# Later weight casts and subtractions, and batch 0's scores and maxima taken around the last residual product, in a gated cross-attention and expert layer

## What is computed

```python
xn = layernorm(x)
k, v = split((ctx @ W_src.T + b_src) * mask)        # 8 heads of 16
q = (xn @ W_tgt.T + b_tgt) * mask
attn = softmax(where(mask == 0, -inf, q k / 4))      # per batch and head
x = x + tanh(g0) * (concat([xn, attn @ v]) @ W_out.T + b_out)
xn2 = layernorm(x)
s = sigmoid(xn2 @ gate.T + bias)                     # 9 experts, 2 taken per token
out = sum over the 2: weight * (silu(xn2 @ w1[e].T) * (xn2 @ w3[e].T)) @ w2[e].T
return x + tanh(g1) * out
```

## Time and profile before

| what | before |
|---|---|
| median of three runs | 217.67 us |
| span of the profiled execution | 234.1 us |
| TensorE busy | 205.4 us, 88% |
| VectorE busy | 149.6 us, 64% |
| ScalarE busy | 142.7 us, 61% |
| POOL busy | 128.8 us, 55% |

### The profile page before, as it was taken

One profiled execution on the slowest core, in us unless ns is written; L12 is line 12 of the kernel. 1 busy time (PEld: TensorE's weight loads), 2 busy tenths in 40 slices (PEclk: granted clock), 3 DMA queues, 4 the chain that ended last, 5 costly groups with the idle time before them and its releaser, 6 DMA issues.

```text
span 234.1 us, 5788 instructions
## 1 busy us (share of the span) xinstructions
PE 205.4 (88%) x1606; PEld 166.9 (71%) x1606; DVE 149.6 (64%) x523; ACT 142.7 (61%) x399; POOL 128.8 (55%) x230
## 2 busy tenths in 40 slices
PE   8999986999999999898883946299999999999981
PEld 3577653666666676565573945299999999999881
DVE  0469997788898698897865822344443444456774
ACT  2286869988778876786471620266667666666210
POOL 4237745132325876786783578556675756557320
PEclk9999999999999999999998897589999999999998
DMA  5999999999910100011372221121222221261194
GB/s 164 368 377 242 407 381 409 408 370 318 342 55 13 36 23 26 23 36 38 86 214 62 61 76 49 41 53 55 61 69 68 52 65 47 49 218 53 37 348 163
DMA packets 23602, 34.91 MB, mean 149 GB/s; under 512 B 2562, under 2 KB 15879, under 8 KB 23443
## 3 DMA queue, kind: packets, MB, share of 16 engines
q1 hardware_dynamic: 20610, 29.27, 37.9%
q0 software_dynamic: 2240, 4.23, 5.5%
q10 hardware_dynamic: 720, 1.02, 1.5%
HBM read 15.85 MB, written 19.06 MB: 149 GB/s over the span
## 4 chain that ended last, share of the span: by engine, by line
PE 56%; DVE 14%; another core or an unknown queue 7%; ACT 6%; DMA 6%; issue 5%; POOL 4%; SPq 1%; POOLq 0%; DVEq 0%; ACTq 0%
PE pt_ps L1363 10%; PE score_ps L1321 5%; PE pt_ps L1372 4%; PE score_ps L1323 4%; PE score_ps L1322 4%; PE score_ps L1176 4%; DMA kheads<-y_rows 3%; PE pt_ps L1116 3%; PE ps_a L1226 3%; PE pt_ps L1214 3%; PE score_ps L1126 2%; PE ps_b L1283 2%; DVE less L827 2%; ACT probs L401 2%
## 5 line engine op out<-in xcount | busy, mean ns | idle before, releaser
L616 POOL DMA_INDIRECT y_rows<-vals,ids x38 | 37.8, 995 | 17.2 <-ACT vals L473 9.6
L1363 PE MATMUL pt_ps<-w,probsT 128*128 x234 | 34.4, 285 | 14.6 <-ACT probsT L480 6.7
L1363 PEld LDWEIGHTS pt_ps<-w,probsT 128*128 128x128 f32 x234 | 32.1, 198 | 15.9 <-issue 15.8
L593 POOL DMA_INDIRECT x_rows<-stage,slot x32 | 32.7, 1022 | 10.4 <-issue 7.7
L401 ACT ACTIVATE probs<-score_ps,less 128x128 f32<-128x128 f32 x128 | 37.9, 419 | 0.4 <-DVE less L827 0.4
L1043 DVE TENSOR_TENSOR xg_low<-ps_a,xg_high 128x128 fp32r<-128x128 f32 x40 | 11.7, 291 | 37.1 <-issue 23.6
L473 ACT ACTIVATE vals<-pt_ps,xg 128x128 f32<-128x128 f32 x38 | 14.0, 368 | 34.4 <-PE pt_ps L1363 24.7
L1321 PE MATMUL score_ps<-w_high,xg_low 128*128 x80 | 30.3, 379 | 0.0
L1051 DVE TENSOR_TENSOR probs<-probs,score_ps 128x352 f32<-128x352 f32 x40 | 20.8, 521 | 11.2 <-PE score_ps L1323 5.3
L1323 PE MATMUL score_ps<-w_high,xg_high 128*128 x80 | 26.6, 332 | 0.0
L1322 PE MATMUL score_ps<-w_low,xg_high 128*128 x80 | 26.5, 332 | 0.0
(11 more groups left out here) (179 smaller groups left out, 445.6 us busy)
## 6 DMA issues: line engine op xcount, KB each, us to landing
x_rows<-pads SPq DMA_DIRECT2D x1, 9945.0 KB, 37.3
w_low<-in_w13T SPq DMA_DIRECT2D x3, 1056.0 KB, 11.0
xg<-x_rows SPq DMA_DIRECT2D x40, 65.0 KB
ctx_r<-in_ctxT SPq DMA_DIRECT2D x4, 512.0 KB, 7.7
y_rows<-pads SPq DMA_DIRECT2D x1, 2048.0 KB, 16.6
w<-in_w2T SPq DMA_DIRECT2D x1, 1728.0 KB, 11.2
kheads<-y_rows SPq DMA_DIRECT2D x3, 512.0 KB, 5.0
mask_b<-in_mask SPq DMA_DIRECT2D x4, 256.0 KB, 8.0
```

The source lines that it names most:

```text
L593: pool.indirect_dma_start(x_rows[:, :], bass.IndirectOffsetOnAxis(ap=slot[:, par, c, p:p + 1], axis=0), stage[:, par, c, p, :], None, boun ...
L616: pool.indirect_dma_start(y_rows[:, :], bass.IndirectOffsetOnAxis(ap=ids[:, s:s + 1], axis=0), yt[:, s, :], None, bounds_check=last_row, o ...
L1363: last = nc.tensor.matmul(into[:, 0:D], hidT[:, q3, c, :], w2[:, bass.ds(e3, 1), c, :].rearrange("p o d -> p (o d)"), start=(c == 0), stop ...
```

## The change

On ScalarE the casts of experts 4 and 5 go into group 3 ahead of the wait for its keys, and those of experts 6, 7 and 8 to the ends of steps 2, 3 and 4. On VectorE no subtraction is left in the projections: experts 0, 1 and 2 are subtracted in step 1, 3 to 7 in steps 2 to 6, and 8 in step 9. In group 3 TensorE computes batch 0's scores between the query product and the residual product. VectorE takes the first half of batch 0's maxima ahead of the residual addition and the second half behind it, and `spread(3)` follows both.

```diff
+LOWS = {1: (0, 1, 2), 2: (3,), 3: (4,), 4: (5,), 5: (6,), 6: (7,), 9: (8,)}
...
+                if j == NG - 1:
+                    high(4)
+                    high(5)
                 act.wait_ge(k_done, j + 2)
...
-                for e in ((), (0, 1), (2, 3), (4, 5, 6))[j]:
+                for e in ((), (0, 1), (2, 3), ())[j]:
                     high(e)
...
-                if k < 2:
-                    high(7 + k)
+                if 2 <= k < NE - 4:
+                    high(4 + k)
...
                 if j + 1 == NG:
-                    spread(j)
+                    maxima(0, 0, 0)
                 dve.wait_ge(r_mm, j + 3)
                 nc.vector.tensor_tensor(xs[:, here, :], bank[3].rearrange("p (b d) -> p b d", b=UN), xs[:, here, :], ALU.add).then_inc(r_done, 1)
-                if j + 1 < NG:
-                    spread(j)
-                if j >= 2:
-                    low(j - 2)
+                if j + 1 == NG:
+                    maxima(0, 0, 1)
+                spread(j)
...
-                if on(k, 0):
+                if on(k, 0) and k > 0:
                     maxima(k, r, 0)
...
-                if 2 + k < NE:
-                    low(2 + k)
+                for expert in LOWS.get(k, ()):
+                    low(expert)
...
                 nc.tensor.matmul(bank[2], w_tgt[:], xn1T[:, r, :], start=True, stop=True).then_inc(q_mm, 1)
+                if j == NG - 1:
+                    pe.wait_ge(v_done, NG + 1)
+                    pe.wait_ge(k_done, NG + 1)
+                    pe.wait_ge(kh_pool, 2 + 2)
+                    pe.wait_ge(kh_dve, 2)
+                    pe.wait_ge(kh_act, 2 + 2)
+                    pe.wait_ge(bias_set, 1 + 2)
+                    all_scores(0, 0)
                 pe.wait_ge(scaled_w, 1)
...
             def step(k, r, i):
-                if k == 0:
+                if k == 1:
                     pe.wait_ge(q_done, NG + 1)
-                if k == 1:
                     pe.wait_ge(r_done, NG + 1)
...
-                if on(k, 0):
+                if on(k, 0) and k > 0:
                     if after(k, 2):
                         pe.wait_ge(prob, 2 * k - 2)
...
+                    all_scores(k, r)
...
-            pe.wait_ge(v_done, NG + 1)
-            pe.wait_ge(k_done, NG + 1)
-            pe.wait_ge(kh_pool, 2 + 2)
-            pe.wait_ge(kh_dve, 2)
-            pe.wait_ge(kh_act, 2 + 2)
-            pe.wait_ge(bias_set, 1 + 2)
             pe.wait_ge(ld_gate, 16)
             turns(step)
```

More of the change, by code:

```diff
@@ L696, in spread, with maxima @@
                 last.then_inc(kh_dve, 1)
+            def maxima(k, r, half):
+                here = slice(half * UN, (half + 1) * UN)
+                dve.wait_ge(scores, 2 * k + half + 1)
+                nc.vector.tensor_reduce(less[:, r % 2, here], score_ps[:, r % 2, here, :], AX.X, ALU.max, negate=True).then_inc(lessened, 1)
             for j in range(NG):
@@ L821, in label_rows @@
                 nc.vector.tensor_copy(slot[:, g % 2], slot_f[:]).then_inc(label_set, 1)
[L823 to L827, removed]
             def unturn(b, q):
@@ L1159, in queries_and_rest, with score_products, score_bias, all_scores @@
                 last.then_inc(r_mm, 1)
+            def score_products(k, r, pair, half):
+                rows, heads = slice(half * RH, (half + 1) * RH), slice(2 * pair, 2 * pair + 2)
+                nc.tensor.matmul(score_ps[:, r % 2, half * HH + 2 * pair:half * HH + 2 * pair + 2, :], qT[rows, k * P:(k + 1) * P],
+                                 kheads[rows, heads, k * P:(k + 1) * P], start=(pair == 0), stop=False, tile_position=(half * RH, 0),
+                                 skip_group_check=True)
+            def score_bias(k, r, half):
+                rows = slice(half * RH, (half + 1) * RH)
+                nc.tensor.matmul(score_ps[:, r % 2, half * HH:(half + 1) * HH, :], share[rows, :],
+                                 bias_b[rows, k * P:(k + 1) * P].unsqueeze(1).to_broadcast([RH, HH, P]),
+                                 start=False, stop=True, tile_position=(half * RH, 0), skip_group_check=True).then_inc(scores, 1)
+            def all_scores(k, r):
+                for pair in range(2):
+                    for half in range(2):
+                        score_products(k, r, pair, half)
+                for half in range(2):
+                    score_bias(k, r, half)
             values(0)
@@ L1171, in _ @@
                 queries_and_rest(j)
-            def score_products(k, r, pair, half):
-                rows, heads = slice(half * RH, (half + 1) * RH), slice(2 * pair, 2 * pair + 2)
-                nc.tensor.matmul(score_ps[:, r % 2, half * HH + 2 * pair:half * HH + 2 * pair + 2, :], qT[rows, k * P:(k + 1) * P],
-                                 kheads[rows, heads, k * P:(k + 1) * P], start=(pair == 0), stop=False, tile_position=(half * RH, 0),
-                                 skip_group_check=True)
-            def score_bias(k, r, half):
-                rows = slice(half * RH, (half + 1) * RH)
-                nc.tensor.matmul(score_ps[:, r % 2, half * HH:(half + 1) * HH, :], share[rows, :],
-                                 bias_b[rows, k * P:(k + 1) * P].unsqueeze(1).to_broadcast([RH, HH, P]),
-                                 start=False, stop=True, tile_position=(half * RH, 0), skip_group_check=True).then_inc(scores, 1)
             def step(k, r, i):
-                if k == 0:
+                if k == 1:
                     pe.wait_ge(q_done, NG + 1)
-                if k == 1:
                     pe.wait_ge(r_done, NG + 1)
```

## The result

The changed kernel takes 215.4 us (median of six runs, 214.43 to 215.48) against 217.88 for the kernel before (six runs). The ratio is 0.9869, with a 95% interval of 0.9847 to 0.9891: 2.85 us faster, where 1.3 had been forecast.

What follows compares the result with a forecast made beforehand. The bound was taken as the VectorE-then-ScalarE chain of waits where projections hand over to attention, with weight work on it. 1.5 us won at scores 3 less 0.2 in step 9 gave 217.67 - 1.3 = 216.4 us, range 215.4 to 217.6.

Steps and rivals of the forecast that it cites:

- Scores 0, residual product, addition, maxima and exponentials: Start of attention: scores 0 at 31.35 not 32.63, exponentials end 1.6 us earlier, scores 2 at 38.1 not 39.88.
- Three subtractions in step 1: VectorE, step 1: they cost 2.75 us (2.4 to 3.6), delay upd's transpose and give back 0.3 at scores 3.
- Rival B: Step 1: subtractions and POOL's v_cur products exclude each other three times; gain only 0.6, 217.1 us; chance 0.22.
- high(8)'s old place: ScalarE, step 1: removing this cast gives 0.1 us at most, since the transposes are as late; taken 0.
- high(6), (7), (8) in steps 2 to 4: Ends of ScalarE's steps: each cast fits the idleness; bounds 0 and 0.67 us per step, taken 0.
- Rival E: Steps 2 to 4 and step 9: weight work is not hidden; net 1.4 us slower, 219.1 us; chance 0.08.
- low(8) in step 9: VectorE, before step 9's x addition: the subtraction costs 0 to 0.87 us, taken 0.2.
- Sum: Whole kernel: 1.5 us won at scores 3, less 0.2 in step 9, gives 1.3 and 216.4 us.
- rival D: VectorE and POOL interleave well, step 9 free, high(8)'s absence counts: gain 1.8 to 2.2 us; chance 0.12.
- Rival C: Expert stage: a stop ending at a fixed moment absorbs the gain, leaving 217.7 us; chance 0.08.

Runs made afterwards that it cites:

- e4: Only the order of scores 0, residual product, maxima and spread(3) changed against the kernel before, casts and subtractions left; ratio 1.0005.
- e3: Casts and subtractions both moved against the kernel before, order of scores and maxima left as it was; ratio 0.9871.
- e1: Only the casts moved against the kernel before: 4 and 5 ahead of group 3's keys, 6 to 8 to steps 2 to 4; ratio 0.9979.
- e8: As e3, but four subtractions in step 1 and none later than step 6; ratio 0.9874 to the kernel before.
- e5: The kernel before run again unedited, for a second profile; 216.64 us, ratio 1.0008.
- e9: Another profile of the unedited kernel before, mean granted clock 0.986; scores 15 at 72.50 us after group 3's key products.
- e10: Another profile of the unedited kernel before, mean granted clock 0.985; scores 15 at 72.34 us after group 3's key products.
- e13: The kernel before with five idle products of 0.25 us added on TensorE in step 1; ratio 0.9967.
- e11: Another profile of the unedited kernel before, mean granted clock 0.987; 187.6 us from group 3's key products to the end.
- e14: Another profile of the kernel with only the order of scores, residual product and maxima changed, mean granted clock 0.987; 218.86 us.

## Why the prediction was wrong

The direction and the mechanism were right: weight work was on the path where attention starts, and once it was off, the gain made there was kept, 1.82 us at scores 3 and 1.89 at scores 15. Two steps failed: the price of high(8), taken as 0, and TensorE's clock, which was no term. The size was short by 1.5 us. By the steps of the prediction:

- *Scores 0, residual product, addition, maxima and exponentials.* Forecast for scores 2: 38.1 - 28.6 = 9.5 after the key products; measured 9.59. The added wait was there too, scores 1 at 6.14 and not 5.68. But the sum credited the new order with part of this, and e4 and e3 show that it earns nothing; kT without low(0) and the exponentials without casts earn it all. The weight transfer came in time: the casts of experts 4 and 5 started at 30.38. (The prediction's 29.9 for it should be 29.5, 17.5 + 12.0.)
- *Three subtractions in step 1.* Forecast 2.75 for the three; measured 2.78, behind a spreading that took 1.11 on VectorE's timeline beside POOL's addition and not the 0.47 of group 2's, with upd's transpose 12.62 after the key products and 12.7 forecast. The Trainium skill (SBUF — State Buffer, "Who interferes with whom") counts tensor_scalar, which the spreading is, among the operations that can take the port pair that VectorE shares with GpSimd; the trace agrees for the spreading. Rival B's three exclusions did not come: POOL's four products ended at 38.33, in the first subtraction. (Its 3.6 was high even so, 3 x 1.16 is 3.5.)

```profile
35.22 1.26 POOL L538 TENSOR_TENSOR xs<-xs,b_resg 128x512 f32<-128x512 f32 x1 [2.23 <-DVE xs L730]
36.45 1.88 POOL L545 TENSOR_TENSOR v_cur<-vals,factors 128x136 f32<-128x136 f32 x4
```

- *high(8)'s old place, "0.1 at most, taken 0".* This term was mis-sized. It is 0.31 by e1. The prediction looked only at the start of the next copy. The rows of the kernel before showed more: behind the cast the copies and the ulT copy were recorded longer, 0.44 for ulT against 0.27 here. Step 2 is 4.28, where the forecast had 4.7: the cast's 0.31 is gone, and the late transpose costs 0.18 (e3's step is 4.10) and not 0.3.
- *high(6), (7), (8) in steps 2 to 4, taken 0.* Right within 0.06: steps of 4.43, 4.37 and 4.37. Rival E did not happen. The step with high(6):

```profile
44.29:48.66 4.37, 4.37 (x44) 2.98 (x42) 3.63 (x9) 4.37 (x15) 1.49 (x5) 1.00 1.02 402
```

ScalarE is now busy 4.37 of 4.37, against 3.82 in the earlier trace rows, and the loop is hardly longer.

- *low(8) in step 9, taken 0.2.* Measured 0, net: 0.18 lost by scores 12 against e8 and 0.22 back in step 12. VectorE still idled 0.31 before the addition, of the 1.11 in the earlier trace rows.

```profile
73.95 0.88 DVE L693 TENSOR_TENSOR w_low<-w_low,w_high 128x704 fp32r<-128x704 f32 x1
75.14 0.29 DVE L870 TENSOR_TENSOR xs<-ps_b,xs 128x128 f32<-128x128 f32 x1 [0.31 <-PE ps_b L1297]
```

- *Sum.* 1.3 forecast, 1.9 in the program: 0.3 is the cast of step 1, 0.2 is low(8), and some 0.1 the rest. This is rival D, 1.8 to 2.2 with step 9 free and high(8)'s absence counted, which had a chance of 0.12.
- *TensorE's clock* was no term at all, and it accounts for most or all of the other 0.9. The prediction took one profiled execution as the kernel, and that one had a granted clock of 1.00 through attention. In 19 of 24 runs the mean is low, at 1.0 to 1.3 us for each low stretch, which makes 0.8 to 1.0 on average. Counted by times it is a little less: the 74 runs of the kernel before average 217.96, the 16 of them without a low mean 217.23, and the 30 with its weight work moved 215.11, so 0.7 goes with the clock and 2.1 does not. The changed kernel keeps TensorE busy 10.0 of the first 11.3 us after the key products started (5.18 + 4.83), where e5 has 8.4 (5.01 + 3.41), and no run of it shows the low mean. That the start of attention is one such place e9 and e10 show; that idleness there is a cause is likely by the counts and by e13, and not proven. Why the changed kernel does not fall at the expert stage either, as e11 and e14 do, is open; it was not tried.
- *Rival C* is out: from scores 15 to the end the changed kernel takes 115.1 and e5 115.0.

## What to carry to other kernels

Work that is needed much later belongs in the idle ends of a steady step and not where one stage hands over to the next; there it sits on the path, and its pieces hide one another: at scores 15 the casts alone earned 0.6 us, the subtractions alone 1.2, and both 2.0. Taking idleness away from TensorE can be worth something beyond the waits themselves, because executions in which its clock falls became fewer with it, so look at the granted clock of every run, not of one profile. And test the parts of a change apart: here the new order of scores, residual product and maxima earned nothing.

## What the runs showed of the hardware

The same program runs at different granted clocks from one execution to the next: the kernel before has runs with means of 0.985, 0.994 and 0.998. In the profiles with a mean of 0.99 and above the clock is low only at the end of the program, behind TensorE's last work (granted clock 0.50 from 212 us to the end at 214.8 in e5, TensorE's last product at 210.8), which costs nothing; those with 0.985 to 0.987 have one low stretch inside as well. Before the falls of e9 and e10 TensorE had been busy 2.81 of 5.0 and 2.66 of 4.9 us, with 1.2 us as its longest single wait; e5 and e11 had the same work and wait there, and the clock stayed at 2.4 GHz. The Trainium skill, TensorE: Matmul & The Clock Gate, Part 1, says that the clock follows how busy the engine has been recently; e13's counts agree, as far as they go.
